# Scores and maxima of attention as float32r products of two exact pieces, two heads at a time in 64-row tiles

## The reference

```python
# layer 1: causal                     # layer 2: ALiBi bias, no mask
scores = q @ k.T / sqrt(8)            scores = q @ k.T / sqrt(8) + slope[h] * min(key - query, 0)
scores = where(causal, -inf, scores)  w = softmax(scores)
out = softmax(scores) @ v             y = w @ v
# layer 3: one more "void" key and value per head, temperature per head
dots = q @ k.T * 128 ** -0.5
out = softmax(dots / temperature) @ v
```

## Time and profile before

| | |
|---|---|
| median of 3 runs | 1177.39 us (1177.02 to 1177.69) |
| span of the profiled execution | 1195.9 us |
| PE busy | 1013.1 us, 85% |
| DVE busy | 779.4 us, 65% |
| ACT busy | 662.2 us, 55% |
| POOL busy | 363.6 us, 30% |
| mean granted TensorE clock | 0.916 of full |

### The profile page before, as it was taken

One profiled execution on the slowest core, in us unless ns is written; L12 is line 12 of the kernel. 1 busy time (PEld: TensorE's weight loads), 2 busy tenths in 40 slices (PEclk: granted clock), 3 DMA queues, 4 the chain that ended last, 5 costly groups with the idle time before them and its releaser, 6 DMA issues.

```text
span 1195.9 us, 18814 instructions
## 1 busy us (share of the span) xinstructions
PE 1013.1 (85%) x6456; PEld 502.9 (42%) x6517; DVE 779.4 (65%) x1614; ACT 662.2 (55%) x1282; POOL 363.6 (30%) x587
## 2 busy tenths in 40 slices
PE   5599789999979899456999999798999998876993
PEld 2267534544436566332333333485323232233551
DVE  5966486768733300388888885429888889646565
ACT  4664536655544345152777777582477776753341
POOL 7535411101532244320000002210112223556554
PEclk9799779999988899865999999898799999999897
DMA  5910224334611120233333220003333423212232
GB/s 142 181 46 1 94 86 144 126 113 129 168 38 36 55 67 18 65 95 126 100 117 125 65 79 5 1 1 126 112 119 119 134 89 96 63 33 62 56 87 80
DMA packets 98374, 101.70 MB, mean 85 GB/s; under 512 B 13354, under 2 KB 80571, under 8 KB 98199
## 3 DMA queue, kind: packets, MB, share of 16 engines
q1 hardware_dynamic: 86169, 89.28, 25.3%
q0 software_dynamic: 6432, 8.18, 2.4%
q10 hardware_dynamic: 5680, 3.04, 0.9%
HBM read 66.60 MB, written 38.09 MB: 88 GB/s over the span
## 4 chain that ended last, share of the span: by engine, by line
PE 67%; DVE 14%; ACT 8%; issue 5%; DMA 3%; another core or an unknown queue 1%; POOL 1%; SPq 0%; ACTq 0%; DVEq 0%; POOLq 0%
PE PS L892 13%; PE PS L876 12%; PE PS L849 8%; PE PS L698 6%; PE PS L703 6%; DVE negm L1663 5%; PE PS L1170 4%; PE PS L1053 3%; PE PS L879 3%; PE PS L1047 2%; PE PS L852 2%; ACT arena L1299 2%; PE PS L900 2%; PE PS L1186 2%; ACT arena L1226 1%
## 5 line engine op out<-in xcount | busy, mean ns | idle before, releaser
L1299 ACT ACTIVATE arena<-PS 128x512 f32<-128x512 f32 (+3 forms) x768 | 363.0, 549 | 190.6 <-PE PS L879 121.8
L1663 DVE TENSOR_REDUCE negm<-PS 128x2 f32<-128x1024 f32 (+3 forms) x384 | 405.2, 1088 | 94.3 <-PE PS L849 46.1
L876 PE MATMUL PS<-arena 128*128 128x512 bf16 (+3 forms) x707 | 221.1, 363 | 12.1 <-ACT arena L1299 8.0
L892 PE MATMUL PS<-arena,VPAD 128*32 128x512 f32 (+3 forms) x1536 | 187.7, 559 | 0.1
L849 PE MATMUL PS<-arena 32*128 32x512 bf16 (+3 forms) x768 | 144.3, 376 | 33.1 <-DVE negm L1663 27.4
L849 PEld LDWEIGHTS PS<-arena 32*128 32x128 bf16 x768 | 36.3, 91 | 216.7 <-DVE negm L1663 112.9
L876 PEld LDWEIGHTS PS<-arena 128*128 128x128 bf16 x768 | 69.9, 98 | 123.5 <-issue 57.3
L2508 POOL CAST nmp<-negm 128x16 bf16<-128x16 f32 x48 | 9.3, 195 | 363.9 <-DVE negm L1663 244.1
L698 PE MATMUL PS<-arena,W 128*128 128x512 f32 x144 | 83.2, 711 | 11.5 <-ACT arena L1217 9.0
L703 PEld LDWEIGHTS PS<-W,arena 128*128 128x128 f32 x640 | 81.0, 206 | 13.8 <-issue 6.3
L703 PE MATMUL PS<-W,arena 128*128 128x128 f32 x640 | 82.8, 291 | 3.3 <-DVE arena L1607 3.0
(11 more groups left out here) (334 smaller groups left out, 1541.3 us busy)
## 6 DMA issues: line engine op xcount, KB each, us to landing
arena<-score_q SPq DMA_DIRECT2D x48, 288.0 KB
arena<-score_k SPq DMA_DIRECT2D x48, 288.0 KB
arena<-max_parts SPq DMA_DIRECT2D x48, 256.0 KB
max_parts<-arena SPq DMA_DIRECT2D x36, 256.0 KB, 2.9
score_k<-arena SPq DMA_DIRECT2D x36, 128.0 KB
score_q<-arena SPq DMA_DIRECT2D x12, 384.0 KB
arena<-rows_y SPq DMA_DIRECT2D x16, 256.0 KB, 4.3
arena<-slots SPq DMA_DIRECT2D x46, 65.0 KB
```

Of the source, the lines that this page charges most:

```text
L876: mm = pe.matmul(PS[:, b, q0:S], OK[s][:, r, kt * P:(kt + 1) * P], OQ[s][:, r, q0:S], start=True, stop=True)
L892: mm = pe.matmul(PS[32 * r:32 * r + 32, 7, q0:S], VP[:, u, kt, r, :], PB[:, kt % 2, r, q0:S], start=(kt == 0), stop=True, skip_group_check ...
L1299: act.activation(PB[:, kt % 2, r, q0:S], PS[:, 4 + use % 3, q0:S], ACT.Exp, scale=slope(u % G, r) if o["slope"] else 1.0).then_inc(exped, 1)
L1663: vec.tensor_reduce(negm[:, u % 2, 2 * rp:2 * rp + 2, qt], PS[:, 2 * (use % 2):2 * (use % 2) + 2, 0:nk], AX.X, ALU.max, negate=True).then_ ...
```

## The change

The operands become float32r, a float32 type for TensorE. Each projected query and key is split in two pieces, its upper 12 significant bits (a bitwise and) and the rest, so that a product has 2 x 2 x 8 = 32 rows (`PRODUCTS`), 8 rows of constants (`NLIN`) and 2 of maxima. 40 rows serve the maxima and 42 the scores, from one operand buffer and one load (`operand_load`). Two heads stand in rows 0 to 63 and 64 to 127, and their products are issued one behind the other as two 64-row tiles. A mask, which was one product of 128 rows with the identity, becomes two of 64 rows for each head. ScalarE's zero fills and its second copy go, as do the maxima's DRAM buffers with the DMAs that filled them at the start. The row of maxima is sent as two DMAs, one for each half. Spills wait for the second piece, and a chunk's first load for all four spills.

```diff
+F32R = mybir.dt.float32r
-NCOMBO = 72
-NLIN = 9
+PRODUCTS, NLIN = 32, 8
+HIGH_BITS = 0xFFFFF000
-PREP_V = "{0}.lo {0}.mid {0}.low {0}.v"
+PREP_V = "{0}.high {0}.low {0}.v"
...
+                self.pieces = view(arena, at + 6144, [2, 2, S])
+        operands = [nc.alloc_sbuf_tensor_at(f"operands{c}", [P, 2, 2, 2, S], F32R, offset=arena_at + 4 * slot_at[2 * c]) for c in range(2)]
+        OQ = [operands[s // 2][:, s % 2, 0] for s in range(NB)]
+        OK = [operands[s // 2][:, s % 2, 1] for s in range(NB)]
...
-        masks = ("causal_kq", "causal_qk", "alibi_kq", "alibi_qk", "tri")
+        masks = ("halves", "causal_kq", "causal_qk", "alibi_kq", "tri")
...
-        mT, rden = sb("mT", [32, NB, P], BF16), sb("rden", [P, R * CT])
+        mT, rden = sb("mT", [32, 2, P], F32R), sb("rden", [P, R * CT])
...
-            def maxima_load(a, u):
-                s, which = u % NB, 1 if ATT[a]["lin"] else 0
-                c, heads = u // G, slice(u % G * R, u % G * R + R)
-                if u % G == 0:
-                    sp.wait_ge(max_spilled[c], 16 * 3 * (a + 1))
-                sp.dma_start(MQK[s], max_parts[which, c, :, :, heads].rearrange("j d r n q -> r (j d) (n q)")).then_inc(max_in[s], 16)
-
-            def score_load(a, u):
-                s, c, heads = u % NB, u // G, slice(u % G * R, u % G * R + R)
+            def operand_load(a, u):
+                s, c = u % NB, u // G
                 if u % G == 0:
                     sp.wait_ge(score_spilled[c], 16 * 4 * (a + 1))
                 if u >= NB:
                     sp.wait_ge(scored, scores_of_unit(a, u - NB))
-                sp.dma_start(OQ[s][0:NCOMBO].rearrange("p r q -> p (r q)"),
-                             score_q[c, :, :, heads].rearrange("i d r q -> (i d) (r q)").unsqueeze(1).broadcast_to([3 * HD, 3, R * S])
-                             ).then_inc(score_in[s], 16)
-                sp.dma_start(OK[s][0:NCOMBO].rearrange("p r q -> p (r q)"),
-                             score_k[c, :, :, heads].rearrange("d j r q -> (d j) (r q)").unsqueeze(0).broadcast_to([3, 3 * HD, R * S])
-                             ).then_inc(score_in[s], 16)
+                for h in range(2):
+                    rows, heads = slice(64 * h, 64 * h + PRODUCTS), slice(u % G * R + 2 * h, u % G * R + 2 * h + 2)
+                    sp.dma_start(OQ[s][rows].rearrange("x p q -> x (p q)").bitcast(F32),
+                                 score_q[c, :, :, heads].rearrange("i d p q -> (i d) (p q)").unsqueeze(1).broadcast_to([2 * HD, 2, 2 * S])
+                                 ).then_inc(score_in[s], 16)
+                    sp.dma_start(OK[s][rows].rearrange("x p q -> x (p q)").bitcast(F32),
+                                 score_k[c, :, :, heads].rearrange("d j p q -> (d j) (p q)").unsqueeze(0).broadcast_to([2, 2 * HD, 2 * S])
+                                 ).then_inc(score_in[s], 16)
...
             def constant_rows(a, c):
-                n = NLIN + 2 if ATT[a]["lin"] else 2
-                sp.wait_ge(blanked[c], a + 1)
...
+                sp.wait_ge(*(T.at(c, "t.sum"), V.at(c, "cb.tot"), T.at(c, "ch.out"))[a])
+                for h in range(2):
+                    rows = slice(64 * h + PRODUCTS, 64 * h + PRODUCTS + NLIN + 2)
...
+            def spills(c, tag, n):
                 sp.wait_ge(*V.at(c, tag + ".low"))
+                for i in range(2):
+                    sp.dma_start((score_q[c, i], score_k[c, :, i])[n], lanes[c].pieces[:, n, i]).then_inc(score_spilled[c], 16)
...
             def spills_and_first_loads(a, tag):
-                max_spills(0, tag, a)
+                for n in range(2):
+                    spills(0, tag, n)
                 constant_rows(a, 0)
-                maxima_load(a, 0)
-                score_spills(0, tag, a)
-                maxima_load(a, 1)
-                score_load(a, 0)
-                score_load(a, 1)
+                operand_load(a, 0)
+                operand_load(a, 1)
                 constant_rows(a, 1)
-                maxima_load(a, 2)
-                score_load(a, 2)
+                operand_load(a, 2)
...
                 def maxima(job):
...
+                    if job in (0, 16):
+                        pe.wait_ge(rows_in[job // 16], 32 * (a + 1))
                     if job % 8 == 0:
-                        pe.wait_ge(max_in[s], 16 * (a * (UNITS // NB) + u // NB + 1))
+                        pe.wait_ge(score_in[s], 64 * (a * (UNITS // NB) + u // NB + 1))
                     nk = (qt + 1) * P if o["causal"] else S
-                    for i in range(2):
-                        rows = slice(32 * (2 * rp + i), 32 * (2 * rp + i) + 32)
-                        mm = pe.matmul(PS[:, b + i, 0:nk], MQ[s][rows, qt * P:(qt + 1) * P], MK[s][rows, 0:nk], start=True, stop=True)
+                    for h in range(2):
+                        rows = slice(64 * h, 64 * h + PRODUCTS + NLIN)
+                        mm = pe.matmul(PS[:, b + h, 0:nk], OQ[s][rows, rp, q], OK[s][rows, rp, 0:nk], start=True, stop=True)
                     if o["qk"]:
-                        for i in range(2):
-                            mm = pe.matmul(PS[:, b + i, qt * P:(qt + 1) * P], bf["ident"][:], bf[o["qk"]][:],
-                                           start=False, stop=True, skip_group_check=True)
+                        for n in range(2):
+                            for h in range(2):
+                                rows = slice(64 * h, 64 * h + 64)
+                                mm = pe.matmul(PS[:, b + h, q], bf["halves"][rows, n], bf[o["qk"]][rows, n],
+                                               start=False, stop=True, skip_group_check=True)
...
                 def scores(job):
...
-                    for i in range(2):
-                        r, b = 2 * rp + i, score_bank(score_use[a, job] + i)
-                        mm = pe.matmul(PS[:, b, q0:S], OK[s][:, r, kt * P:(kt + 1) * P], OQ[s][:, r, q0:S],
-                                       start=True, stop=True)
-                        if o["kq"]:
-                            mm = pe.matmul(PS[:, b, kt * P:(kt + 1) * P], bf["ident"][:], bf[o["kq"]][:],
-                                           start=False, stop=True, skip_group_check=True)
-                        mm.then_inc(scored, 1)
+                    b, mm = [], []
+                    for h in range(2):
+                        rows = slice(64 * h, 64 * h + PRODUCTS + NLIN + 2)
+                        b.append(score_bank(score_use[a, job] + h))
+                        mm.append(pe.matmul(PS[:, b[h], q0:S], OK[s][rows, rp, kt * P:(kt + 1) * P], OQ[s][rows, rp, q0:S], start=True, stop=True))
+                    if o["kq"]:
+                        for n in range(2):
+                            for h in range(2):
+                                rows = slice(64 * h, 64 * h + 64)
+                                mm[h] = pe.matmul(PS[:, b[h], kt * P:(kt + 1) * P], bf["halves"][rows, n], bf[o["kq"]][rows, n],
+                                                  start=False, stop=True, skip_group_check=True)
+                    for h in range(2):
+                        mm[h].then_inc(scored, 1)
...
-            def blank_rows(a, c):
-                act.wait_ge(*PO.at(WHOLE, "zeros"))
-                act.wait_ge(*(T.at(c, "t.sum"), V.at(c, "cb.tot"), T.at(c, "ch.out"))[a])
-                act.copy(view(arena, lanes[c].big, [2 * R * S]), zeros[:, 0:1].broadcast_to([P, 2 * R * S])).then_inc(blanked[c], 1)
-
             def operand(c, tag, n, scale, bias):
...
-                act.activation(L.parts[:, n, 0, :], bank(b), ACT.Identity, scale=scale, bias=bias)
                 act.activation(L.pair[:, n, :], bank(b), ACT.Identity, scale=scale, bias=bias).then_inc(*A.did(c, f"{tag}.{part}"))
...
             def splits(c, tag):
                 L = lanes[c]
                 vec.wait_ge(*A.at(c, tag + ".k"))
-                vec.tensor_tensor(L.pair, L.pair, L.parts[:, :, 0, :], ALU.subtract).then_inc(*V.did(c, tag + ".lo"))
-                vec.wait_ge(*V.at(c, tag + ".lo"))
-                vec.tensor_copy(L.parts[:, :, 1, :], L.pair).then_inc(*V.did(c, tag + ".mid"))
-                vec.wait_ge(*V.at(c, tag + ".mid"))
-                vec.tensor_tensor(L.parts[:, :, 2, :], L.pair, L.parts[:, :, 1, :], ALU.subtract).then_inc(*V.did(c, tag + ".low"))
+                vec.tensor_scalar(L.pieces[:, :, 0].bitcast(U32), L.pair.bitcast(U32), HIGH_BITS, None, ALU.bitwise_and).then_inc(*V.did(c, tag + ".high"))
+                vec.wait_ge(*V.at(c, tag + ".high"))
+                vec.tensor_tensor(L.pieces[:, :, 1], L.pair, L.pieces[:, :, 0], ALU.subtract).then_inc(*V.did(c, tag + ".low"))
...
-                    pool.dma_start(OQ[s][KR:KR + 2].rearrange("a r (t q) -> a (r t) q", t=CT), mT[:, s, :]).then_inc(max_row[s], 16)
+                    for h in range(2):
+                        at = 64 * h + PRODUCTS + NLIN
```

(1 more changed line is left out.)

143 lines of the change are left out of this document (47 added, 96 removed).

## The result

The changed kernel takes **1309.5 us** (median of four runs, 1292.9 to 1322.8) where the kernel before takes 1177.2: a ratio of 1.1055 [1.0983, 1.1126]. The forecast was 1172.4, with 1205 as its upper end. A second measurement of the same kernel (e13) gave 1324.6 beside 1196.2, 1.1041 [1.0989, 1.1093]. The profiled execution took 1312.31 us (span 1311.0).

What follows compares the result with a forecast made beforehand. It took the attentions to be bound by a chain of scores, exponential and bank wait hidden in TensorE's busy time. Preparation -8, first attention +7, second -1, third -4, row of maxima +1 gave -5 us: 1172.4, range 1165 to 1182.

Steps and rivals of the forecast that it cites:

- a granted clock that falls in the attentions because TensorE now idles in each slot: Sign named as making the forecast wrong, in the three attentions; given no size and no chance.
- the term of the slots: Slot work in the three attentions: +7 us in the first, -1 in the second, -4 in the third.
- 2.91 and 2.68: Predicted us per two slots in the second and third attention, where the kernel before took 2.95 and 2.78.
- +0.40: First attention: each unit of eight slots gets 0.40 us longer, over 16 units; with 0.5 at the end, +7.
- that 0.11: Spacing in us of 128-column float32 transpose records, taken as the time of a float32r product's load of weights.
- the fills: ScalarE's zero fills: two on the chain before the first attention count whole when removed, -7.0 us.
- The splits: Operand splitting on VectorE: 1.0 us saved each, twice before the first attention, once before each other one: -4.0.
- rival (a): Half masks or 128-column products cost double: +11 us in the second, +14 in the first attention, about 1190; chance 0.18.
- rival (b): Float32r products stream in more than one pass; two passes add 108 us, giving 1285; chance 0.10.
- (c): TensorE's relief counts if the exponential's bank wait did not bind; VectorE sets the pace: -50 us, 1128; chance 0.08.
- Rival (d): First operand loads are wide, so the second and third attention start 3 us earlier each: 1168; chance 0.09.
- The row of maxima: First attention: lands 4.7 us after issue; a second 0.6 us issue uses up 0.7 us to spare: +1 us.

Runs made afterwards that it cites:

- e13: The changed kernel itself measured a second time, nothing altered: 1324.6 us beside 1196.2 of the kernel before, ratio 1.104.
- e14: Changed kernel with zeros in rows 42 to 63 of each 64-row tile and maxima and score products over all 64 rows: ratio 1.065 to the kernel before.
- e11: Changed kernel with zeros in rows 42 to 63, products over all 64 rows, and each k load issued as two wide ones: ratio 1.039 to the kernel before.
- e4: Changed kernel with each k load issued as two, one per copy, instead of one with a leading repeat of two: 1298.3 us, ratio 1.085.
- e9: Kernel before with fills kept and score products reading 83 rows (74 without position rows) instead of 128: ratio 1.0164.
- e1: Changed kernel with every product of maxima and scores issued twice: 1422.2 us, ratio 1.181 to the kernel before.
- e3: Changed kernel with maxima and scores reading the upper halves of the same float32r words as bf16: 1237.8 us, ratio 1.036 to the kernel before.
- e12: Changed kernel with 64 rows read, wide k loads and operands read as bf16: ratio 1.005 to the kernel before.
- e18: Kernel before with ScalarE's zero fills replaced by transfers of zeros, late on SP's queue under their own semaphore, constant rows early: 1168.3 us beside 1178.3, ratio 0.9917.
- e6: Changed kernel with each mask added by one 128-row product per head instead of two half-height steps (masks wrong): ratio 1.182 to the kernel before.
- e15: Kernel before with zero fills replaced by transfers of zeros, these and the constant rows issued behind the maxima's loads of unit 1: ratio 1.0005.
- e16: e15 with four bf16 128-row products ahead of each of the 14 early maxima of the second and third attention: ratio 1.0002 to the kernel before.
- e17: e15 with maxima's loads of units 1 and 2 ahead of the zeros, second chunk's zeros behind unit 1's score loads: ratio 1.0017 to the kernel before.
- e2: Changed kernel with both heads of a slot on the first 64-row tile, one after the other: 1746.5 us, ratio 1.459 to the kernel before.
- e7: e4 with 48 bf16 products of 128 rows in the wait for first operands of the second and third attention: 1272.1 us, ratio 1.084.

## Why the prediction was wrong

**The step that failed is that the sum took every unit of the attentions at full granted clock**, as the earlier trace rows show it for the middle of two attentions before. The first units of each attention, which those rows leave out, stood below it already, at 0.87, 0.71 and 0.72. The text named "a granted clock that falls in the attentions because TensorE now idles in each slot" as what would make it wrong, and gave it no price. It is 69 of the 113 us that the attentions got longer, 73 of 117 in e13.

The reason that it gave is refuted: e14 idles in each slot as the changed kernel does and has a clock of 0.90 instead of 0.83. What the runs show instead is that the rows in use count. Three pairs of runs differ in them and keep the products: e14 against e13 (1.065 for 1.104, 47 us), e11 against e4 (1.039 for 1.085), and e9 against the kernel before (+1.6%). The earlier trace rows could have warned: products of 128 rows, of which 54 hold zeros there, and 45 where the position rows are in use. The forecast counted the products' time and never their rows. Rows aren't the only cause. With 40 and 42 rows the clock also rose when the products were issued twice (e1, 0.87) and when they were bf16 (e3, 0.87), and e4's second attention came to full clock as early as e14's.

**Second, the term of the slots was mis-sized, by the operands' type.** The forecast has +2 us for the slots (7 - 1 - 4), and at full clock they took 44: 0.25 a pair in the second attention, 0.20 in the third, 1.0 a unit in the first over their bf16 form. With bf16 (e3, e12) the slots' arithmetic holds: pairs 2.93 and 2.70 for 2.91 and 2.68, first attention +0.2 a unit for +0.40, and 3 us in all. That it is the load of weights is read from the records, not tried by itself: "The load of its weights I take at that 0.11 too, which the streams of 384 and 512 columns cover."
**Right in place:** the fills. Without them the first attention starts 6 to 10 us earlier than in the profile of before (forecast 7), but only 2 to 5 earlier than in e9, which has them; e18's 10 us of the whole are the firmer figure. The splits take 0.70 and 1.24 for three steps of 3.14, -1.2 each (forecast -1.0):

```profile
574.39 0.70 DVE arena L1482
575.12 1.24 DVE arena L1484
```

That holds for the second attention. The first split of all, ahead of the first attention's spills, takes 1.99 and 2.17 us (123.36 to 127.55) and took 2.25, 0.69 and 1.23 before (127.67 to 131.91): nothing was won by it, where the forecast has -1.0.

The first attention's exponentials stand in pairs 0.2 apart, and the evacuation comes 0.25 later in its unit. Before, where the unit's first exponential is at 204.12, then after:

```profile
206.11 0.59 ACT L1312 COPY arena<-PS 128x512 f32<-128x512 f32 x1
```

```profile
237.09 1.09 ACT L1261 ACTIVATE arena<-PS 128x512 f32<-128x512 f32 x2 [0.44 <-PE PS L848]
238.36 1.09 ACT L1261 ACTIVATE arena<-PS 128x512 f32<-128x512 f32 x2 [0.18 <-PE PS L848]
239.33 0.59 ACT L1274 COPY arena<-PS 128x512 f32<-128x512 f32 x1
```

Half masks run side by side (rival (a), e6). The product has one pass (rival (b), 0.23). That TensorE's relief counts by itself (c) is refuted by the bank wait, which is still there in e12. Rival (d) had the loads the wrong way round. The row of maxima lands sooner than before, 2.3 us against 4.7 in the earlier trace rows:

```profile
DMA to landing us min/median/max: 1.9/2.3/6.5
```

Two sums of the forecast are off by 1 to 2 us and decide nothing: -0.04 for 57 pairs and +0.1 for seven is -1.6, put down as -1, and rival (d) comes to 1166.4, not 1168.

**Open:** what besides the rows sets the clock, as e1, e3 and e4's second attention show that something does; why e6's clock is lower than the changed kernel's; why single units late in the first and third attention are low in every version of the changed kernel; and what makes the stage behind the third attention last 127 or 140 us.

## What to carry to other kernels

Before a product is made smaller, ask what it does to TensorE's clock: rows of zeros that look like waste can be what holds it, as in e9 and e14, and a change should be priced with stretches at both levels. Where TensorE wakes from a wait, no other product hides the next weight load, and the operand type can have a price, here 41 us. When a fill or load is moved to a queue, follow everything that waits on the same semaphore or stands behind it: three of five versions (e15, e16, e17) gave the whole gain back there. And where one stage differs by 12 us, see whether the same kernel profiled again shows it too.

## What the runs showed of the hardware that was not expected

Rows filled with zeros count: 64 instead of 42 rows in each of two tiles brought the mean granted clock from 0.83 to 0.90, and 83 instead of 128 took it from 0.915 to 0.89. A TensorE that is busy in every microsecond can stay at the lower level for hundreds of them (e2, 0.50 from 300 to 500 us). And 48 dense products ahead of an attention did not bring its first units to full clock: in e7 the level fell again in the thin stretch of maxima behind them, and those units took longer than in e4, which lacks the products.
